# Scores nine steps behind the row products instead of eleven, row maxima turned one step sooner, the first unit's sent from ScalarE's queue

## The reference

```python
q, k, v = split_heads(x_n @ Wq + bq), split_heads(ctx @ Wk + bk), split_heads(ctx @ Wv + bv)
s = einsum('bhqd,bhkd->bhqk', q, k) / sqrt(d)
s = where(causal_or_key_mask, s, -inf)          # attention 0: both, 1: strict causal, 2: keys, 3: causal, 4: none
o = einsum('bhqk,bhkd->bhqd', softmax(s, axis=-1), v)
x = x + tanh(g_xattn[l]) * (merge_heads(o) @ Wo + bo)
```

## Time and profile before

| what | value |
|---|---|
| median of three runs | 1301.71 us |
| span of the profiled execution | 1299.6 us |
| TensorE matmul busy | 987.3 us, 76% |
| VectorE busy | 874.6 us, 67% |
| ScalarE busy | 673.6 us, 52% |
| GpSimd busy | 454.9 us, 35% |
| row products of the five attentions start at | 42.65, 226.57, 658.90, 921.15, 1055.98 us |
| their first score products start at | 63.05, 241.37, 681.21, 938.89, 1072.56 us |
| their last exponential ends at | 157.29, 326.93, 774.67, 1026.87, 1168.58 us |

### The profile page before, as it was taken

How to read it: one execution, slowest core, us unless ns; L and a number is a source line. 1 busy time by engine, 2 the same in 40 slices (tenths; PEclk the granted TensorE clock), 3 DMA queues, 4 the chain that set the end, 5 groups by cost and what they waited for, 6 DMA issues and landing times. The chain is left out here.

```text
span 1299.6 us, 29076 instructions
## 1 busy us (share of the span) xinstructions
PE 987.3 (76%) x10092; PEld 503.4 (39%) x10092; DVE 874.6 (67%) x1801; ACT 673.6 (52%) x1316; POOL 454.9 (35%) x572
## 2 busy tenths in 40 slices
PE   3678857888479999999757786281788677785997
PEld 2334544545334444444322245260444432233342
DVE  4668745887668677676669977163778678963453
ACT  2157612477245555555418861160367427873886
POOL 3105301453235555555503531305003101211886
PEclk9879958899789999999879995595889987996999
DMA  7731202310044444444271100211611051101332
GB/s 216 255 133 36 62 1 76 107 52 3 1 101 131 130 134 124 129 122 133 64 259 39 35 2 9 83 61 34 228 36 36 2 164 34 35 2 29 100 94 73
DMA packets 110893, 109.34 MB, mean 84 GB/s; under 512 B 16139, under 2 KB 86995, under 8 KB 109747
## 3 DMA queue, kind: packets, MB, share of 16 engines
q1 hardware_dynamic: 107460, 92.32, 24.0%
q10 hardware_dynamic: 2288, 13.31, 2.8%
q0 software_dynamic: 1024, 2.10, 0.6%
HBM read 83.83 MB, written 23.53 MB: 83 GB/s over the span
## 5 line engine op out<-in xcount | busy, mean ns | idle before, releaser
L762 ACT ACTIVATE work<-ps 128x384 f32<-128x384 f32 (+1 forms) x640 | 303.8, 533 | 167.2 <-PE ps L618 106.4
L861 DVE TENSOR_REDUCE bmax<-ps 128x6 f32<-128x768 f32 (+1 forms) x320 | 335.6, 1056 | 61.2 <-PE ps L596 46.1
L1669 POOL TENSOR_TENSOR work<-Ks,work 128x512 f16<-128x512 f32 x196 | 227.1, 1159 | 167.5 <-ACT work L1757 162.1
L1682 PE MATMUL ps<-ao,wf 128*128 128x512 f16 x984 | 249.0, 385 | 8.1 <-DVEq L1781 4.3
L1805 DVE TENSOR_TENSOR Ks<-ps,Qs 128x512 f32<-128x512 f32 x192 | 132.7, 692 | 55.5 <-ACT ps L1749 43.7
L607 PE MATMUL ps<-Qs,Ks 32*128 32x256 f16 x640 | 122.5, 291 | 55.7 <-issue 20.7
L1698 PE MATMUL ps<-work,wf 128*128 128x512 f16 x588 | 159.2, 380 | 2.5 <-POOL work L1669 2.5
L899 POOL TENSOR_SCALAR mx<-bmax 128x16 f16<-128x16 f32 x80 | 25.0, 313 | 373.3 <-DVE bmax L867 220.2
L640 PE MATMUL ps<-work,V 128*9 128x256 f32 (+1 forms) x2560 | 155.6, 363 | 0.0
L1682 PEld LDWEIGHTS ps<-ao,wf 128*128 (+1 forms) x984 | 89.3, 99 | 141.5 <-issue 44.9
L1749 ACT ACTIVATE work<-ps 128x512 f32<-128x512 f32 x132 | 78.9, 598 | 115.7 <-PE ps L1682 110.2
(11 more groups left out here) (256 smaller groups left out, 1538.1 us busy)
## 6 DMA issues: line engine op xcount, KB each, us to landing
Qs<-scrC SPq DMA_DIRECT2D x256, 128.0 KB, 3.0
Qs<-scrQ SPq DMA_DIRECT2D x40, 256.0 KB, 3.1
Ks<-scrK SPq DMA_DIRECT2D x40, 256.0 KB, 3.4
Qs<-scrC SPq DMA_DIRECT2D x32, 256.0 KB, 3.2
scrK<-work SPq DMA_DIRECT2D x60, 128.0 KB, 2.2
scrQ<-work SPq DMA_DIRECT2D x60, 128.0 KB, 2.6
Qs<-mxT SPq DMA_DIRECT2D x320, 1.0 KB
wf<-in_L_w ACTq DMA_DIRECT2D x2, 1792.0 KB, 9.5
```

The lines of the kernel that those rows point to most:

```text
L762: act.activation(prob[:, g % 8, 0:W1], ps[:, 4 + g % 3, 0:W1], ACT.Exp, scale=float(att["dk"]) ** -0.5).then_inc(exped, 1)
L861: dve.tensor_reduce(bmax[:, n // 4 % 2, 2 * (n % 4):2 * (n % 4) + 2, 0:NB], ps[:, b0:b0 + 2, 0:W1].rearrange("p i (n w) -> p i n w", n=NB) ...
L1669: pool.tensor_tensor(hparts[:, (m + r) % 4, 1, :], weighted(m + r), hparts[:, (m + r) % 4, 0, :], ALU.subtract).then_inc(second, 1)
L1682: ins = pe.matmul(out, weight_parts(which, wpart, j), xh[:, xpart, c * CH:(c + 1) * CH], start=(i == 0), stop=(i == 2))
```

## The change

`LEAD` becomes 9, so the head has nine steps, both products stand in steps 9 to 63, and the tail is steps 64 to 72. `turn_step`, `ring_places` and the warm matmuls (steps 5 to 8) follow from it. VectorE transposes the maxima in steps 4, 8, 12, ... Unit 0's four DMAs are issued on ScalarE's queue, ahead of its waits for the writes and of the expert loads; SyncE sends units 1 to 15.

```diff
-LEAD = 11
+LEAD = 9
@@
+    def maxima_rows(u):
+
+        b, half = u // 2, u % 2
+        return Qs[25:128:32, b % 4, 2 * half:2 * half + 2, :].rearrange("i a (c b r) -> i b (a c) r", c=2, b=4)
@@ scalar
+            act.wait_ge(max_turned, 1)
+            rows_of = maxima_rows(0)
+            for k in range(4):
+                act.dma_start(rows_of[:, k], mxT[32 * k:32 * k + 4, 0]).then_inc(max_in[0], 16)
             for k in range(4):
                 act.wait_ge(written[k], 96)
@@ vector
-                if n >= 5 and n % 4 == 1 and (n - 5) // 4 < NUNIT:
-                    turn_maxima((n - 5) // 4)
+                if n >= 4 and n % 4 == 0 and (n - 4) // 4 < NUNIT:
+                    turn_maxima((n - 4) // 4)
@@ sync
-                if n >= 6 and n % 4 == 2:
+                if n >= 10 and n % 4 == 2:
                     maxima((n - 6) // 4)
```

More of the change, by code:

```diff
@@ L958, in maxima @@
                 sp.wait_ge(max_turned, u + 1)
-                b, half = u // 2, u % 2
-                rows_of = Qs[25:128:32, b % 4, 2 * half:2 * half + 2, :].rearrange("i a (c b r) -> i b (a c) r", c=2, b=4)
+                rows_of = maxima_rows(u)
                 for k in range(4):
```

## The result

The changed kernel takes 1313.83 us (median of 6 runs, 1308.79 to 1318.66) against 1302.28 for the kernel before (6 runs, 1301.61 to 1307.46): ratio 1.0067, interval 1.0043 to 1.0091 (the quotient of the two medians would be 1.0089). It is slower, by 0.4 to 0.9%. The forecast was 1293.0, faster. The profiled execution has 1313.9 us of span (before 1299.6), so 14.3 us have to be found. Of the later kernel with output 2 alone moved, two of twelve runs fell in a slower state of the chip, and its median and ratio are those of the other ten.

A forecast was written before the change was run, and what follows sets the result against it. The steady loop was taken as full, with the waste at each attention's start: 12.75 us of earlier starts less 2.2, 1.1 and 0.8 gave 8.65 net, so 1290.95 us of span and 1293.0 measured; range 1286.5 to 1299.

The forecast's parts named there:

- Two more steps with both products, two fewer in the tail: Each attention: +2.62 or 2.88 us for two more double steps, tail -1.62, idle up to -1.2; 2.2 us for five.
- the tail as long as before: Sign of being wrong: the steps after the last scores get no shorter, though 1.62 us of work leaves them per attention.
- Unit 0, by ScalarE's queue: Start of attentions: first scores earlier by 2.4 us in attention 1, 2.25 in attention 4; in attention 0 possible at 55.1.
- Unit 1, in the flood: Attentions 0, 2 and 3: unit 1's first score, its DMAs caught among expert loads, comes 2.9, 2.4 and 2.8 us earlier.
- rival A: Attention 0's unit 1 waits for all the expert loads; the gain is 2.9 us less, 1295.9 us; chance 0.15.
- The steady part: Middle of each attention: five steps from transposition to score suffice, no new wait, 0 us; 1.31 and 1.44 us a step unchanged.
- The zero fill: Attention 0's unit 13: scores come about one step sooner behind the fill's landing, so a new wait costs 1.1 us.
- The clock: Start of scores: earlier work may fall into the 1.2 GHz stretch, as in attention 2; +0.8 us, bounds -3 and +4.
- B: The two extra double steps (3 us) and a longer slow clock (4 us) give the gain back; about 1299 us; chance 0.12.
- C: Maxima come too late in every unit of the causal attentions, TensorE waiting each fourth step; 1304 to 1314 us; chance 0.07.

The follow-up runs named there:

- the repeated trace: The changed kernel run once more without alteration, beside later kernels: 1314.63 us, ratio 1.0089 to the kernel before.
- the sending alone: The changed kernel with LEAD back at 11, keeping the sooner transposition and unit 0's DMAs on ScalarE's queue: 1297.68 us, ratio 0.9944 to the kernel before.
- the pair with pieces: The changed kernel with expert weights in pieces on SyncE's queue behind the maxima, without and with outputs in steps 64, 66 and 70: 1295.69 and 1290.69 us.

## Why the prediction was wrong

**The step that failed** is "Two more steps with both products, two fewer in the tail". Its two halves are two terms, and the first was right: from score product 52 to the last row reduction each attention takes 2.65 to 3.1 us more, where 2.62 and 2.88 were forecast. The second was to give back 1.62 us and up to 1.2 of idle time. It gave back none. From the last row reduction's end to the last copy it took 21.5, 21.1, 22.1, 21.1, 22.0 us before and takes 21.6, 21.7, 22.5, 21.2, 21.0, with two score steps fewer. The pair cost 14.6 us (-0.7 + 15.3), not 2.2 (2.5 by the prediction's own terms, since the middle for attentions 2 and 4 is 0.66). The prediction's own sign of being wrong, "the tail as long as before", is what came. The prediction counted the work that leaves the tail and did not ask where the tail's last stretch would then begin. The outputs' steps are counted from the row products (64, 68, 72), the last score product moved from step 74 to 72, onto output 2. Its transposes, its projection and VectorE's statistics then stand between the last scores and the last division. The order of the program shows this, and the experiments show that the place of the outputs costs time: made in the kernel before it costs 12.0 us, and moving output 2 alone takes the changed kernel from 1.0089 to 0.998. It isn't the whole of the 12.4 us by which the term was off. In the stretch itself the better place gives back 5.4 to 5.9. With both outputs moved the tail is 5.7 us shorter in five attentions, where the removed work alone was put at 8.1; so the other half is work and idle time that were counted as gain and gave none.

In attention 3 two of the idle 0.40 us were covered, but that was worth nothing, since TensorE then waited for the exponentials. An idle gap tells that work can be put there, not that the stretch gets shorter by it.

**Unit 0, by ScalarE's queue: right.** 13.33 us behind the row products' start in attention 0, 12.45 forecast (55.1 - 42.65); 1.7 us earlier in attention 1 (2.4), 1.9 in attention 4 (2.25). The 0.4 to 0.9 us missing are mostly the issue, 3.10 us instead of 2.4.

**Unit 1, in the flood: the size right, by luck in attention 0.** The five starts give 9.7 us in one trace and 15.0 in the other of the changed kernel; 12.75 were forecast. In attention 0 score product 4 stands 25.7, 26.0, 28.0, 30.7 and 31.6 us behind the first row product in five traces with the same sending and nine steps (the last with more idle matmuls). With 29 forecast, no single trace could have told the prediction from rival A. What they do tell is the mechanism. In the repeated trace unit 1's scores start at 67.33, and the last load, issued at 57.16, lands 17.7 us later, at 74.9:

```profile
57.16 0.48 ACTq L441 DMA_DIRECT2D wf<-in_L_wd  x1
...
67.33 0.36 PE L612 MATMUL ps<-Qs,Ks 32*128 32x256 f16 x1 [4.98 <-issue]
...
wf<-in_L_wd ACTq DMA_DIRECT2D x1, 2112.0 KB, 17.7
```

So unit 1 isn't held to the flood's end, and rival A is out; by the Trainium skill (DMA: Bandwidth & Descriptors, Queues, rings and completion order) that is the reading in which the engines take turns between queues. The price of a turn is not a constant, though: it varied by 6 us over four transfers.

**The steady part: right.** 272.1 us against 272.4, and the five steps are enough even with the later transposition. **The zero fill:** attention 0's unit 13 comes 6.10 us behind unit 12 instead of 5.49, 0.6 where 1.1 was forecast (in the repeated trace 0.9, and 0.8 more at unit 14).

**The clock: too small.** +0.8 was forecast, with +4 as its bound; the first stretch of scores took 7.4 us more (8.0 in the repeated trace, 6.4 in the sending alone). The prediction had one attention in mind, attention 2; it was attentions 1 and 2 in the first trace, and all five by 0.5 to 2.2 us in the repeated one. An earlier start is not enough for it: attention 1's scores started 1.7 us earlier, and its clock came back 8.1 us later. What decides when it comes back, no run here shows. With the 9.7 us gained ahead of it, only 2.3 of the changed kernel's start were left.

**Rivals.** B came nearest in kind: the two extra steps and the clock give it back. But its price, 3 us for the steps, missed the end too. C had the right time, 1314, for a reason that no trace shows. The chance of slower, 0.06, was low because all terms but one could only be small; the one was never bounded from above by the worst placement of the tail's work.

**Open.** Moving the outputs is worth 15 us or so in two pairs, and 5.0 in the third. From score product 52 to the last copy it gives 5.9, 5.4 and 4.4. The stretches between the attentions are 5 us shorter in all three pairs (the first of them by 2.5, 1.2 and 4.1), and the heads and the end of the program differ by up to 9 either way. That goes with the clock: behind the last attention the program is the same and VectorE equally busy, and the traces of the changed kernel again and of output 2 sooner have

```profile
1183.12:1313.53 130.41, 110.62 (x474) 47.31 (x474) 54.84 (x100) 86.49 (x143) 78.46 (x68) 0.85 0.26 74
...
1174.25:1296.04 121.79, 102.42 (x474) 42.91 (x474) 54.84 (x101) 86.28 (x143) 78.40 (x68) 0.93 0.30 79
```

Between attentions 0 and 1 the length follows the time at 1.2 GHz in all fourteen traces, from 61.3 us with 32.5 of it at 1.2 GHz to 67.0 with 44.7. Whether the outputs' place moves the clock or the executions differ by chance isn't settled, since no run could hold the clock fixed. An estimate from the runs' own clocks: among the runs of one kernel 0.01 less mean granted clock goes with about 5 us, and the mean clock was 0.866 for the changed kernel again, 0.875 with output 2 moved, and 0.876 and 0.878 in the pair with pieces. So about 4 of the 15.9 us and 1 of the 5.0 go with the clock, which leaves some 11 and 4.

## What to carry to other kernels

When a loop's lag is changed, list what is placed by the other loop's count and see what comes to stand behind the last item: the end of a pipeline is priced by the chain behind its last item, not by the work taken out. An idle gap on one engine isn't time to be won until you have asked what that engine waits for next. Small transfers on which the pipeline waits and megabytes for later don't go out together; cut the large ones into pieces behind the small ones, and then look for who waits for the last piece. And repair the ends before judging a lag: nine and eleven steps came out equal once both were.

## What the runs showed of the hardware

- Four 1 KB transfers issued beside three loads of 2112 KB on another queue: the score that waited for them started 7 to 17 us after their issue. With the same bytes in pieces on one queue behind them, it started without a wait, 11 us sooner (19.66 us behind the first row product, 30.67 before).
- ScalarE takes 3.10 us to issue four such DMAs, 1.18 for the first; SyncE takes 2.25 to 2.41, beside the loads too.
- The time until TensorE's clock returns to 2.4 GHz once the scores have begun differs between executions of the same program: 28.5 and 15.4 us in attention 2 of the changed kernel. More matmuls ahead of it did not shorten it: with them the stretches at 1.2 GHz were 335 us instead of 304 in one pair, with about 1% more time, and 382 beside 352 and 365 in the other, with no clear difference in time.
